# Attention scores of a gated cross-attention kernel: one fp32 product per head, or three fp32r products of split operands

## The reference

```python
q = (hidden_states @ q_proj_w.T).reshape(B, Q, NUM_HEADS, HEAD_DIM).transpose(0, 2, 1, 3)
k = (cross_attention_states @ k_proj_w.T).reshape(B, KV, NUM_KV_HEADS, HEAD_DIM).transpose(0, 2, 1, 3)
v = ...
q = rmsnorm(q, q_norm_w)
k = rmsnorm(jnp.repeat(k, n_rep, axis=1), k_norm_w)
v = jnp.repeat(v, n_rep, axis=1)
scores = jnp.einsum('bhqd,bhkd->bhqk', q, k) * scale + attention_mask
attn = jax.nn.softmax(scores, axis=-1)
out = jnp.einsum('bhqk,bhkd->bhqd', attn, v)
out = out.transpose(0, 2, 1, 3).reshape(B, Q, NUM_HEADS * HEAD_DIM) @ o_proj_w.T
x = x + jnp.tanh(g_xattn[0]) * out
```

## Time and profile before

| what | us |
|---|---|
| device time, median of 2 runs | 795.81 (793.47 to 798.14) |
| profiled execution, its own time | 799.69 |
| its span in the trace | 797.8 |
| TensorE busy | 751.3 (94%) |
| VectorE, ScalarE, GpSimd busy | 468.2, 485.4, 310.7 |
| mean granted TensorE clock | 0.98 of full speed |

### The profile page before, as it was taken

One profiled execution on the slowest core, in us unless ns is written; L12 is line 12 of the kernel. 1 busy time (PEld: TensorE's weight loads), 2 busy tenths in 40 slices (PEclk: granted clock), 3 DMA queues, 4 the chain that ended last, 5 costly groups with the idle time before them and its releaser, 6 DMA issues.

```text
span 797.8 us, 13672 instructions
## 1 busy us (share of the span) xinstructions
PE 751.3 (94%) x3975; PEld 610.2 (76%) x3975; DVE 468.2 (59%) x893; ACT 485.4 (61%) x1818; POOL 310.7 (39%) x622
## 2 busy tenths in 40 slices
PE   5999988999999999999999999999999987987997
PEld 3788876888888887888888788888888633566775
DVE  4785404565656564656565565555666664787653
ACT  4543327767676766676667667676666466556831
POOL 0331015353444453445354335354423438524242
PEclk9999999999999999999999999999999999796999
DMA  8545461303303313032132130330430145664232
GB/s 298 183 133 171 132 188 68 120 19 115 134 14 120 111 36 120 14 119 79 66 120 77 69 120 13 119 133 13 129 105 2 53 120 178 242 253 147 82 108 77
DMA packets 42126, 87.78 MB, mean 110 GB/s; under 512 B 5561, under 2 KB 26041, under 8 KB 38226
## 3 DMA queue, kind: packets, MB, share of 16 engines
q1 hardware_dynamic: 38884, 78.71, 29.0%
q0 software_dynamic: 3184, 8.41, 3.1%
HBM read 70.28 MB, written 35.57 MB: 133 GB/s over the span
## 4 chain that ended last, share of the span: by engine, by line
PE 70%; DVE 6%; ACT 4%; issue 2%; DMA 1%; POOL 1%; POOLq 0%; ACTq 0%; DVEq 0%
PE banks L860 7%; PE banks L862 7%; PE banks L861 7%; PE banks L832 7%; PE banks L831 7%; PE banks L830 7%; PE banks L820 6%; PE banks L839 4%; PE banks L847 3%; PE banks L1771 2%; PE banks L1772 2%; PE banks L1773 2%; PE banks L873 2%; PE banks L871 2%; PE banks L872 2%
## 5 line engine op out<-in xcount | busy, mean ns | idle before, releaser
L575 ACT ACTIVATE p_sb<-p_sb,nmax 128x128 f32<-128x128 f32 x256 | 99.7, 390 | 131.9 <-DVE nmax L748 131.9
L669 POOL TENSOR_TENSOR v_lo<-v_raw,v_hi 128x128 fp32r<-128x128 f32 x64 | 29.6, 462 | 253.3 <-ACT v_hi L613 253.3
L771 DVE TENSOR_TENSOR pT_lo<-banks,pT_hi 128x512 fp32r<-128x512 f32 x64 | 44.3, 692 | 49.8 <-ACT pT_hi L588 49.8
L820 PEld LDWEIGHTS banks<-kT,qT_sb 128*128 128x128 f32 x512 | 66.8, 191 | 6.7 <-ACT qT_sb L583 1.8
L820 PE MATMUL banks<-kT,qT_sb 128*128 128x128 f32 x512 | 67.5, 275 | 1.4 <-ACT qT_sb L583 1.4
L674 POOL TENSOR_TENSOR p_sb<-p_sb,rsum 128x512 f32<-128x512 f32 x64 | 66.6, 1041 | 5.3 <-DVE rsum L767 5.3
L620 ACT ACTIVATE q_junk<-banks 128x128 f32<-128x128 f32 x256 | 66.1, 273 | 3.4 <-PE banks L832 3.4
L739 DVE TENSOR_TENSOR oT_lo<-banks,oT_hi 128x512 fp32r<-128x512 f32 x64 | 44.1, 689 | 35.6 <-ACT oT_hi L570 35.5
L398 PE MATMUL banks<-w_hi,ctx_hi 128*128 128x512 f32 x128 | 53.7, 420 | 8.3 <-DVE ctx_lo L329 8.2
L777 DVE SCALAR_TENSOR_TENSOR x_sb<-banks,tgates,x_sb 128x512 f32<-128x512 f32 x64 | 48.1, 751 | 17.2 <-PE banks L862 15.8
L570 ACT ACTIVATE oT_hi<-banks 128x512 fp32r<-128x512 f32 x64 | 38.0, 594 | 31.6 <-PE banks L873 27.4
(11 more groups left out here) (274 smaller groups left out, 2112.3 us busy)
## 6 DMA issues: line engine op xcount, KB each, us to landing
sorted_x<-in_empty SPq DMA_DIRECT2D x8, 2064.0 KB, 9.2
w_raw<-in_wq_l SPq DMA_DIRECT2D x8, 1024.0 KB, 5.6
w_raw<-in_wo_l SPq DMA_DIRECT2D x8, 1024.0 KB, 4.8
exp_w<-in_exp_w_l SPq DMA_DIRECT2D x8, 1024.0 KB, 9.4
kT_scr<-kT_st SPq DMA_DIRECT2D x16, 256.0 KB, 2.3
v_scr<-v_st SPq DMA_DIRECT2D x16, 256.0 KB, 2.4
xs<-sorted_x SPq DMA_DIRECT2D x15, 258.0 KB, 3.0
v_raw<-v_scr SPq DMA_DIRECT2D x14, 256.0 KB, 2.5
```

What stands on the lines that cost most here:

```text
L575: last = act.activation(p_sb[:, b % 2, h * P:(h + 1) * P], p_sb[:, b % 2, h * P:(h + 1) * P], ACT.Exp, bias=nmax[:, b % 2, h:h + 1], accum ...
L820: last = pe.matmul(s_ps[:, h * P:(h + 1) * P], qT_sb[:, b % 2, h * P:(h + 1) * P], kT[:, b * P:(b + 1) * P], start=True, stop=True)
```

## The change

The scores of a head become three fp32r products over split operands. The keys are split once per unit: ScalarE writes `k_hi`, GpSimd `k_lo`, two units ahead. The transposed queries are split as they leave PSUM: ScalarE writes `qT_hi` (in the place of `qT_copy`), VectorE `qT_lo`, behind `pT_split` in its order. The scores wait for `qT_lo_done` and `k_lo_done` of their unit, the next `q_transpose` waits for `qT_lo_done`, and the DMA that reloads a half of `kT` waits for the key splits instead of the scores.

```diff
-        qT_sb = m.sb("qT_sb", [P, 2, D])
+        k_hi = m.sb("k_hi", [P, 4, P], F32R)
+        k_lo = m.sb("k_lo", [P, 4, P], F32R)
+        qT_hi = m.sb("qT_hi", [P, 2, D], F32R)
+        qT_lo = m.sb("qT_lo", [P, 2, D], F32R)
...
                 def kT_half(c):
-                    reached(sp, s_done, 8 * g - 4 + 4 * c)
+                    reached(sp, k_hi_done, 8 * g - 4 + 4 * c)
+                    reached(sp, k_lo_done, 8 * g - 4 + 4 * c)
...
-            def qT_copy(u, b, g, odd):
+            def qT_split(u, b, g, odd):
                 act.wait_ge(qT_done, u + 1)
                 reached(act, s_done, u - 1)
-                act.activation(qT_sb[:, b % 2, :], qT_ps[:, :], ACT.Copy).then_inc(qT_copied, 1)
+                act.activation(qT_hi[:, b % 2, :], qT_ps[:, :], ACT.Copy).then_inc(qT_hi_done, 1)
+
+            def k_split(u, b, g, odd):
+                reached(act, kT_ld[b // 4], 16 * g)
+                reached(act, s_done, u - 3)
+                act.activation(k_hi[:, b % 4, :], kT[:, b * P:(b + 1) * P], ACT.Copy).then_inc(k_hi_done, 1)
...
-            run(act, [(oT_split, -2), (exps, 0), (copy_z01, 0), (qT_copy, 1), (pT_split, -1), (copy_xT, -4), (copy_z23, -2),
-                      (v_split, 2), (q_stats, 2), (seed_ln2, -3), (split_bias, 0)]
+            run(act, [(oT_split, -2), (exps, 0), (copy_z01, 0), (qT_split, 1), (pT_split, -1), (copy_xT, -4), (copy_z23, -2),
+                      (v_split, 2), (k_split, 2), (q_stats, 2), (seed_ln2, -3), (split_bias, 0)]
...
+            def k_split(u, b, g, odd):
+                pool.wait_ge(k_hi_done, u + 1)
+                pool.tensor_tensor(k_lo[:, b % 4, :], kT[:, b * P:(b + 1) * P], k_hi[:, b % 4, :].bitcast(F32),
+                                   ALU.subtract).then_inc(k_lo_done, 1)
...
-            run(pool, [(v_split, 2), (normalize, 0), (q_rstd, 2), (rstd_ln2, -3)]
+            run(pool, [(v_split, 2), (k_split, 2), (normalize, 0), (q_rstd, 2), (rstd_ln2, -3)]
...
+            def qT_split(u, b, g, odd):
+                dve.wait_ge(qT_hi_done, u + 1)
+                dve.tensor_tensor(qT_lo[:, b % 2, :], qT_ps[:, :], qT_hi[:, b % 2, :].bitcast(F32), ALU.subtract)\
+                    .then_inc(qT_lo_done, 1)
...
-            run(dve, [(oT_split, -2), (mask_max, 0), (normalise_ln2, -4), (q_scale, 1), (p_recip, 0), (pT_split, -1), (q_half, 2),
+            run(dve, [(oT_split, -2), (mask_max, 0), (normalise_ln2, -4), (q_scale, 1), (p_recip, 0), (pT_split, -1), (qT_split, 1), (q_half, 2),
...
             def scores(u, b, g, odd):
-                pe.wait_ge(qT_copied, u + 1)
-                if b % 4 == 0:
-                    reached(pe, kT_ld[b // 4], 16 * g)
+                pe.wait_ge(qT_lo_done, u + 1)
+                pe.wait_ge(k_lo_done, u + 1)
                 reached(pe, masked, u)
                 for h in range(HG):
-                    last = pe.matmul(s_ps[:, h * P:(h + 1) * P], qT_sb[:, b % 2, h * P:(h + 1) * P],
-                                     kT[:, b * P:(b + 1) * P], start=True, stop=True)
+                    out = s_ps[:, h * P:(h + 1) * P]
+                    qh, ql = qT_hi[:, b % 2, h * P:(h + 1) * P], qT_lo[:, b % 2, h * P:(h + 1) * P]
+                    pe.matmul(out, qh, k_hi[:, b % 4, :], start=True, stop=False)
+                    pe.matmul(out, qh, k_lo[:, b % 4, :], start=False, stop=False)
+                    last = pe.matmul(out, ql, k_hi[:, b % 4, :], start=False, stop=True)
                 last.then_inc(s_done, 1)
...
             def q_transpose(u, b, g, odd):
                 pe.wait_ge(q_scaled, u + 1)
-                reached(pe, qT_copied, u)
+                reached(pe, qT_lo_done, u)
```

More of the change, by code:

```diff
@@ L474, in attention @@
         half_done = m.sem("q_half_done")
-        qT_done, qT_copied = m.sem("qT_done"), m.sem("qT_copied")
+        k_hi_done, k_lo_done = m.sem("k_hi_done"), m.sem("k_lo_done")
+        qT_done, qT_hi_done, qT_lo_done = m.sem("qT_done"), m.sem("qT_hi_done"), m.sem("qT_lo_done")
         s_done, masked, max_done = m.sem("s_done"), m.sem("masked"), m.sem("max_done")
@@ L878, in transpose_x @@
                     pe.wait_ge(q_scaled, UNITS)
-                    pe.wait_ge(qT_copied, UNITS)
+                    pe.wait_ge(qT_lo_done, UNITS)
                     pe.wait_ge(masked, UNITS)
```

## The result

The changed kernel took 830.66 us (median of 2 runs, 827.25 and 834.07), before 795.81: ratio 1.0414 (95% interval 1.036 to 1.0468). The profiled execution took 827.25 us, with a span of 825.3.

A forecast was written before the change was run, and what follows sets the result against it. TensorE, issuing products without waits in steady units, was taken as the bound. 64 x 0.446 = 28.5 us for scores loads plus 1.4 at the start gave 29.9, on 795.8, rounded up to 826; range of 8 in 10: 809 to 843.

The forecast's parts named there:

- The price of a product: Scores on TensorE: each fp32r product of 128 columns costs its weight load, 0.1115 us, with the columns hidden beneath.
- The size: Whole kernel: 28.5 us for the scores in 64 units plus 1.4 at the start, 29.9 us in all.
- The term of 1.338 us per unit: Scores on TensorE: twelve loads of 0.1115 us in place of 0.892 us, +0.446 per unit.
- The query split: VectorE's new subtraction, 0.69 us: hidden in steady units, 1.4 us ahead of scores; 1.4 us for the first two scores.
- The key split: ScalarE's extra copy, 0.20 us, and GpSimd's 0.46 us: both cost nothing, as the keys are ready two units ahead.
- What bounds the kernel: Steady units: TensorE issues products without waits, so its changes appear whole in the time, 64 times.
- The sentence that the others have 2.5 us and more of slack per unit: Steady units of 7.95 us: engines other than TensorE were taken to have that much room.
- not slower, 784: Scores on TensorE: cost follows moving columns alone, 0.057 us per product, -13.5 us, +1.4 for the start; 3%.
- Skipped loads: Scores on TensorE: the load of an unchanged qT_hi is skipped, +14.5 + 1.4 us, 812; 6%.
- A narrow fp32r product at the price of an fp32 one: Scores on TensorE: not one pass, so the change triples the scores, +114 + 1.4 us, 911; 13%.
- The middle value: Scores on TensorE: load and product overlap better, 0.084 us per product, +7.4 + 1.4 us, 805; 3%.
- Late elementwise work: VectorE and ScalarE: `qT_lo` or `oT_hi` comes late and scores or q_transpose wait, 839, up to 872; 7%.

The follow-up runs named there:

- e_cols64: Changed kernel with twelve scores products of 64 moving columns instead of 128, scores incomplete: 829.53 us, ratio 1.0389 to the kernel before.
- e_four: Changed kernel with a fourth product per head, low part times low part, 16 per unit: 861.91 us, ratio 1.0823 to the kernel before.
- e_wide: Changed kernel with keys as weights, three products of 512 columns per unit, softmax over the wrong axis: 799.44 us, ratio 1.0036 to the kernel before.
- e_fp32split: Changed kernel with all splits and waits kept, but one plain fp32 product per head: 801.87 us, ratio 1.0063 to the kernel before.
- e_hihi: Changed kernel with one fp32r product per head, both corrections left out: 801.93 us, ratio 1.0051 to the kernel before.
- the runs with the new order: VectorE scales the next queries ahead of mask and maximum: kernel before 812.65 us; changed kernel with one product per head 826.87, with three wide products 825.61.

## Why the prediction came out right, step by step

**The price of a product.** Right in its size, and the columns are excluded as its cause. The steady distance is 0.11 us with 128 columns, with 64 (e_cols64) and with sixteen products instead of twelve (e_four, 0.1115 each in time), and the same arithmetic in three wide products costs half (e_wide). What the earlier trace rows showed after a standstill, that a load keeps the next one off for 0.11 us, is the price of the row of short products. That it is the load and no other fixed price of such a product is what the rows suggest, with no run that shortens the load. The Trainium skill ("TensorE: Matmul & The Clock Gate", LDWEIGHTS) says the same with P/1.2 ns, 107 ns for 128 columns; these runs agree, with 0.11 us. The Trainium skill's figure of about 81 ns per product at 128 columns ("TensorE: Matmul & The Clock Gate", Back-to-back issue gap) isn't borne out by the 112 ns here.

**The size.** The term of 1.338 us per unit measured 1.353, which is 1 us of the total. The other part of what was missing was no term of mine: the long products beside the scores are slower than before by some 0.04 us per unit, mean of the alternating units, 2.7 us in all. Together it is 0.504 instead of 0.446 per unit, 3.7 of the 4.4 us between forecast and measurement.

**The query split.** In steady units hidden as said, 1.25 us ahead instead of 1.4. At the start the wait grew by 1.4 us as said, but the first three steps cost 3.3 us beyond the products, not 1.4: the granted clock fell to 0.50 in them, in both traces of the changed kernel, and the prediction, which looked at the wait alone, had no term for that. It also had none for the 1.9 us that the turns of the loop and the last steps gave back. That these two cancel is luck.

**The key split.** Free in the changed kernel, but ScalarE's slack was misread. I let its work keep its place while the unit grew. It moved along with TensorE, as the query copy now waits for q_transpose (39 times between 200 and 600 us, 0.17 us each), and `oT_hi` idles 0.24 us, not 0.57. e_fp32split shows what that is worth without the longer products: 0.2 us in each step with two weight splits.

**What bounds the kernel.** The sentence that the others have 2.5 us and more of slack per unit failed. Sums of busy time say so, but a loop of waits stood at 7.85 beside TensorE's 7.93 (e_hihi, e_wide), and ScalarE's own at about 7.7 (an estimate from the runs with the new order). The forecast didn't need it, because the change lengthened TensorE's part. The rival "not slower, 784" would have: even with scores at 0.68 per unit, e_wide took 799. That wrong sentence would have spoiled a forecast of any gain here, and it did spoil my expectation of e_hihi by 32 us.

**The rivals.** Skipped loads: excluded by e_four. A narrow fp32r product at the price of an fp32 one: excluded, 0.1127 instead of 0.223. The middle value: excluded. Late elementwise work: not in steady units of the change, though it is near (e_fp32split).

**Left open.** Why the neighbours are slower. It isn't the splits as such, which leave them alone in e_fp32split. With four short products (e_hihi) the products of q_proj stand 0.228 apart again, as in the kernel before, with twelve of 64 columns (e_cols64) 0.229, with twelve or sixteen of 128 columns 0.232. So it goes with the short products, but doesn't grow from twelve to sixteen. Open too is why two of the twelve traces with the longer wait at the start keep the full clock behind it.

## What to carry to other kernels

Before a product is replaced by several cheaper ones, count weight loads, not passes: look for a load behind a standstill and take its distance to the next one as the least that such a product costs, and make the operand that is shared the weights, with the wide one moving. When an added wait makes TensorE stand still longer, look at the granted clock behind it too. Before a gain is forecast from an engine that is busy all the time, add up the loop of waits through the other engines once around the unit; the nearest one stood here 0.07 us below, and neither a shorter product nor a new order came past it. Look also at the steps that aren't steady, since they ate even that 0.07. What came past was the version that took stages out of the loops (maximum, transposes, normalising), after which TensorE went through its unit without a wait.

## What was not expected of the hardware

- VectorE's reciprocal is slow per element: 3.36 us for 128x512, where a product of two tensors of that size took 0.68. On ScalarE a logarithm took 0.59 and an exponential 0.63.
- fp32r products of 512 columns stand 0.227 us apart in e_wide and 0.232 in the changed kernel's q_proj, with the granted clock at 0.99 and above. In o_proj of the changed kernel their mean alternates from unit to unit, which makes the units 8.41 and 8.45.
